# Pair products moved over the loop edge, and a triangular solve by 64x64 blocks in place of the last inversion level

## The chip, the cores and the metric

The kernel runs on one core of one Trainium2 chip. Its time is the device time of one execution, in microseconds. TensorE multiplies matrices, VectorE, ScalarE and GpSimd work on elements, and SyncE issues the transfers between HBM and the core's memory. Each engine works through its own queue in order and waits on semaphores that the others raise.

## The reference

Sixteen sequences of 256 tokens with 128 features pass through two modulated layers. Each layer is an attention-like part and a feed-forward part, both behind a layer norm with shift and scale. In layer 0 these are a selective scan (called `a_` in the kernel) and routed experts (`b_`). In layer 1 they are a gated delta rule with 8 heads (`c_`) and softmax attention with 8 gated experts (`d_`). The change touches the delta rule:

```
def step(S, inp):
    q_t, k_t, v_t, g_t, b_t = inp
    S = S * jnp.exp(g_t)[..., None, None]
    u = (v_t - jnp.einsum('bhk,bhkv->bhv', k_t, S)) * b_t[..., None]
    S = S + jnp.einsum('bhk,bhv->bhkv', k_t, u)
    o_t = jnp.einsum('bhk,bhkv->bhv', q_t, S)
```

The kernel does not step through the tokens. It takes them in two chunks of 128. In a chunk, the vectors `u` of one head solve a system with a 128x128 unit triangular matrix that is made of pair products of keys and of decays. The right-hand side has 32 columns a head.

## The kernel before

The work of one sequence is cut in two. `FIRST_HALF` is the scan, the routed experts and the projections of the delta rule, with the pair products at its end. `SECOND_HALF` is the inversion, its application, the attention and the experts. The loop runs over the sequences, 15 turns: one turn does the first half of sequence i and the second half of sequence i-1. Ahead of the loop stands the first half of sequence 0, behind it the second half of the last sequence. Each engine has a string in `TURNS`, written out by a planner ahead of time, which says for each of its steps whether the next one is of the first half (x) or of the second (y). So the order on an engine is fixed, and a step that waits holds up all that is behind it.

The steps around the change, with their lines:

* `c_gmask` (GpSimd, L552) makes masked decays for a group of four heads; there are four groups. `c_logd` (TensorE, L962) sums them into bank 2, ScalarE takes the exponential (L701), `c_prod` (TensorE, L976) multiplies keys with keys and queries into banks 0 and 1, VectorE multiplies by the decays (L1489, L1491), and `c_unit` (GpSimd, L563, L564) puts ones on the diagonal.
* `c_first` (VectorE, L1499) makes the inverses of the 2x2 blocks. Then six levels double the size of the inverted blocks, from 2 to 128. For both chunks (0 and 1) in turn, a level is a transpose (`lev_T`, VectorE, L1508; the first one L1505), a product of 64x64 tiles (`lev_Z`, L984), an eviction with a mask (L1513), a second product (`lev_TT`, L984) and a copy (ScalarE, L719). The last level works on the block off the diagonal alone, through a full 128x128 inverse `TTf` (L722, L711, L724, L992, L1006, L1019, L1517).
* `c_X` multiplies the whole inverse by the right-hand side `R` (`per_head`, L1034), `c_U` scales it, `c_O`, `c_S` and `c_kS` use it; the second chunk needs the state that the first one leaves.
* `a_norm` to `a_step` prepare the scan. Its eight steps are `drive` (VectorE, L1332), the scan (L1344) and a read (L1352). For each, TensorE spreads one row of B into bank 0 and one of C into bank 1 (L832) and adds up pairs of states (L855), and ScalarE makes the decays (L634).
* `keep_warm` (L1026) are two products whose result nobody reads. They stand ahead of waits of TensorE.

Of the kernel before, what the change touches and what calls it, by code (L numbers as in the profile page):

```python
# [9 lines left out]
ALU = mybir.AluOpType  # L10
ACT = mybir.ActivationFunctionType
# [24 lines left out]
LEVELS = [2, 4, 8, 16, 32, 64]  # L36
# [14 lines left out]
C_GT = C_MERGE + HALF * (len(LEVELS) - 1)  # L51
# [13 lines left out]
def constants():  # L65
# [28 lines left out]
PROJECT = [("c_norm",), ("c_norm2",), ("c_turn",), ("c_ba",), ("c_beta",), ("c_soft",), ("c_soft2",), ("c_gmask", 0), ("c_gmask", 1)]  # L94
PROJECT += [("c_proj", m) for m in range(12)]
PROJECT += [("c_gate",)]
PROJECT += [("c_turn_k", 0), ("c_turn_k", 1), ("c_scales",), ("c_turn_v",), ("c_decay",)]
for gr in range(GROUPS):
    PROJECT += [("c_logd", gr), ("c_prod", gr, 0), ("c_prod", gr, 1), ("c_unit", gr)]
    if gr + 2 < GROUPS:  # L100
        PROJECT += [("c_gmask", gr + 2)]
PROJECT += [("c_roots",)]
# [5 lines left out]
APPLY = [("c_R", 0), ("c_X", 0), ("c_U", 0), ("c_O", 0), ("c_S",), ("c_o", 0), ("c_kS",), ("c_R", 1), ("c_X", 1),  # L108
# [15 lines left out]
SECOND_HALF = INVERT + APPLY + ATTEND + EXPERTS  # L124
# [29 lines left out]
def build(nc, a, out, NB):  # L154
    with ExitStack() as ctx:
# [63 lines left out]
        unit_gate = sb("unit_gate", [P, GROUPS])  # L219
# [58 lines left out]
        gmask = [wide[:, 3, 512 * n:512 * n + 512].rearrange("p (h t) -> p h t", t=P) for n in range(2)]  # L278
        et = [wide[:, 4, 512 * n:512 * n + 512].rearrange("p (h t) -> p h t", t=P) for n in range(2)]
# [21 lines left out]
        inv = sb("inv", [P, 12, 512])  # L301
        TTd = [inv[:, n].rearrange("p (h t) -> p h t", t=HALF) for n in range(2)]
# [31 lines left out]
        released = sem("inversion_step_released")  # L334

# [154 lines left out]
        def _(g):  # L490
# [5 lines left out]
            g.memset(TTf[:], 0.0)  # L496
# [83 lines left out]
        def _(s):  # L580
# [116 lines left out]
            def c_logd(i, gr):  # L697
# [3 lines left out]
                s.activation(et[gr % 2].rearrange("p h t -> p (h t)"), bank(2), ACT.Exp).then_inc(c_et.h, 1)  # L701
# [5 lines left out]
            def lev_T(i, l, ch):  # L707

                if l + 1 == NL:
                    s.wait_ge(c_Tp.h, c_Tp.at(i, ch + 1))  # L710
                    s.copy(TN[ch][0:HALF].rearrange("p h t -> p (h t)"), PS[0:HALF, 5 + ch, :]).then_inc(c_Tl.h, 1)  # L711

            def lev_TT(i, l, ch):
                if l + 2 < NL:
# [3 lines left out]
                if l + 2 < NL:  # L718
# [61 lines left out]
        def _(t):  # L780
# [908 lines left out]
```

## Time and profile before

| what | value |
|---|---|
| median of 3 runs | 3085.35 us (3083.61 to 3086.35) |
| profiled execution | 3073.01 us |
| its span | 3071.2 us |
| TensorE busy | 2502.6 us (81%) |
| VectorE busy | 2245.6 us (73%) |
| ScalarE busy | 1247.8 us (41%) |
| GpSimd busy | 641.2 us (21%) |
| mean granted TensorE clock | 0.906 |

The span goes from the first to the last instruction. The busy share is that of an engine over the whole span. Stretches of one turn of the loop have different limits, so the share alone does not say what a step costs.

### The profile page before, as it was taken

Reading aid. Unit: us, or ns where it says so; the run is one execution under the profiler, and the core shown is the slowest. Engines: PE = TensorE matmul, PEld = TensorE weight load, DVE = VectorE, ACT = ScalarE, POOL = GpSimd, SP = SyncE. Lnnn points to the kernel's source line nnn. Section 1 sums busy time; section 2 is a strip of 40 time slices with the busy share of each in tenths; the row PEclk is TensorE's granted clock in tenths of the full one; section 3 lists DMA queues with packets and bytes.
Section 4 is the critical chain, followed back from the end, with each engine's and each line's share of the span. In section 5 each row is a group of like instructions: output and inputs, shape, how many; then the busy total and the mean of one; then the engine's idle time right before and its main releaser. Section 6 shows DMA issues by size and latency. Waiting matters only on the chain.

```text
span 3071.2 us, 61542 instructions
## 1 busy us (share of the span) xinstructions
PE 2502.6 (81%) x22808; PEld 2004.1 (65%) x22808; DVE 2245.6 (73%) x5056; ACT 1247.8 (41%) x2761; POOL 641.2 (21%) x528
## 2 busy tenths in 40 slices
PE   2477978879887887978889797887988788897897
PEld 1166766757766576766757676575766657676686
DVE  1668777787877778787687877778787777877762
ACT  0233533435344253533425353243534424353342
POOL 0222122131212222122131212313121122202210
PEclk9869989989899898989989998998989989898998
DMA  4000000000000000000000000000000000000000
GB/s 119 2 2 3 2 8 3 7 3 7 2 3 8 2 7 3 6 2 3 7 3 7 2 3 8 3 7 3 7 2 3 7 3 7 3 4 5 1 5 2
DMA packets 24718, 21.52 MB, mean 7 GB/s; under 512 B 7210, under 2 KB 21443, under 8 KB 24403
## 3 DMA queue, kind: packets, MB, share of 16 engines
q1 hardware_dynamic: 24402, 17.14, 2.0%
q8 instruction: 219, 3.59, 0.5%
q14 instruction: 97, 0.79, 0.1%
HBM read 15.00 MB, written 2.13 MB: 6 GB/s over the span
## 4 chain that ended last, share of the span: by engine, by line
PE 60%; DVE 18%; issue 13%; POOL 4%; ACT 3%; SPq 1%; DMA 1%; DVEq 0%; POOLq 0%; ACTq 0%
PE banks L984 8%; PE banks L1160 8%; PE banks L1150 8%; PE banks L1034 6%; PE banks L918 4%; PE banks L927 3%; DVE wide L1332 3%; PE banks L976 3%; DVE wide L1344 2%; PE banks L855 2%; PE banks L962 2%; PE banks L1019 2%; PE banks L1026 2%; PE banks L897 2%; POOL lg L536 2%
## 5 line engine op out<-in xcount | busy, mean ns | idle before, releaser
L532 POOL TENSOR_TENSOR wide<-wide 128x512 f32<-128x512 f32 x128 | 243.5, 1902 | 872.5 <-DVE wide L1352 560.7
L1461 DVE SCALAR_TENSOR_TENSOR wide<-pad,conv,wide 128x256 f32<-128x256 f32 x864 | 389.1, 518 | 0.0
L984 PE MATMUL banks<-inv,mats 64*64 64x64 f32 x5120 | 198.0, 237 | 141.8 <-DVE inv L1505 104.6
L1344 DVE TENSOR_TENSOR_SCAN wide<-wide 128x1024 f32<-128x1024 f32 x128 | 308.4, 2409 | 1.9 <-ACT wide L634 0.3
L634 ACT ACTIVATE wide<-small,a_neg 128x255 f32<-128x255 f32 x512 | 217.8, 497 | 201.8 <-DVE wide L1344 198.9
L984 PEld LDWEIGHTS banks<-inv,mats 64*64 64x64 f32 x5120 | 185.2, 152 | 160.1 <-issue 159.2
L1150 PE MATMUL banks<-inv,up 128*128 128x256 f32 x1024 | 264.9, 387 | 0.0
L1160 PE MATMUL banks<-down,inv 128*128 128x128 f32 x2048 | 257.7, 277 | 0.0
L768 ACT ACTIVATE inv<-banks,up1b 128x256 f32<-128x256 f32 x512 | 215.0, 481 | 105.0 <-PE banks L1150 104.8
L1160 PEld LDWEIGHTS banks<-down,inv 128*128 128x128 f32 x2048 | 249.9, 192 | 5.8
L984 PE MATMUL banks<-inv 64*64 64x64 f32 x5120 | 189.0, 233 | 29.0 <-DVE inv L1513 28.9
L719 ACT COPY inv<-banks 128x512 f32<-128x512 f32 x128 | 74.7, 584 | 333.3 <-DVE inv L1508 332.4
L984 PEld LDWEIGHTS banks<-inv 64*64 64x64 f32 x5120 | 177.3, 147 | 47.9 <-issue 47.4
L1150 PEld LDWEIGHTS banks<-inv,up 128*128 128x128 f32 x1024 | 178.9, 191 | 17.8
L832 PE MATMUL banks<-bc,sel3b 96*128 96x256 bf16 x512 | 104.5, 307 | 83.5 <-DVE wide L1352 59.9
L1026 PE MATMUL banks<-hideb,identb 128*128 128x512 bf16 x512 | 171.6, 420 | 0.0
L855 PE MATMUL banks<-wide,con 128*128 128x512 f32 x256 | 142.8, 653 | 34.0 <-POOL wide L532 34.0
L1332 DVE TENSOR_TENSOR wide<-banks,small 128x1024 f32<-128x1024 f32 x128 | 153.9, 1202 | 19.5 <-PE banks L832 19.5
L563 POOL TENSOR_TENSOR unit_gate<-con 128x1 f32<-128x1 f32 x64 | 12.4, 194 | 732.4 <-DVE mats L1489 732.4
L1352 DVE TENSOR_TENSOR wide<-banks,wide 128x1024 f32<-128x1024 f32 x128 | 155.5, 1215 | 0.5
L1513 DVE TENSOR_TENSOR inv<-banks,con 128x512 f32<-128x512 f32 x160 | 107.2, 686 | 57.4 <-PE banks L984 57.4
L1489 DVE SCALAR_TENSOR_TENSOR mats<-banks,negc,wide 128x128 f32<-128x128 f32 x256 | 77.4, 344 | 98.1 <-PE banks L976 98.1
(281 smaller groups left out, 5160.1 us busy)
## 6 DMA issues: line engine op xcount, KB each, us to landing
gates_bc<-gate_rows SPq DMA_DIRECT2D x32, 128.0 KB, 2.9
up<-in_W SPq DMA_DIRECT2D x1, 2048.0 KB
x<-in_x SPq DMA_DIRECT2D x16, 128.0 KB, 2.1
out<-xn_y SPq DMA_DIRECT2D x16, 128.0 KB, 1.9
wide<-in_wmod SPq DMA_DIRECT2D x2, 384.0 KB
con<-in_con SPq DMA_DIRECT2D x1, 724.0 KB
w_k<-in_Wk SPq DMA_DIRECT2D x1, 512.0 KB
w_q<-in_Wq SPq DMA_DIRECT2D x1, 512.0 KB
```

The costliest lines, as they stand in the source:

```text
L532: g.tensor_tensor(ypart[p % 2], r[:, 0:512], r[:, 512:1024], ALU.add).then_inc(a_yp.h, 1)
L634: last = s.activation(decay[st % 2][:, at + 1:at + T], dt[:, c, 1:T], ACT.Exp, scale=a_neg[:, c, st * SG + q:st * SG + q + 1])
L768: s.activation(hm[e % 2][:, m, :], bank(3 + half, T, q * T), ACT.Relu, bias=up1b[:, HB1 * e + m:HB1 * e + m + 1]).then_inc(d_hid.h, 1)
L855: t.matmul(bank(2), ident, ypart[st % 2], start=st == 2, stop=st == NG + 1).then_inc(a_yq.h, 1)
L984: last = t.matmul(PS[a:b, out, h * HALF:(h + 1) * HALF], weights(h, a, b), values(h, a, b), start=True, stop=True)
L1026: t.matmul(bank(bk), identb[:], hideb[:].unsqueeze(1).broadcast_to([P, HG, P]), start=True, stop=True)
L1034: last = t.matmul(bank(bk, width, first), weights(h), flat[:, first:first + width], start=True, stop=True)
L1150: last = t.matmul(bank(3 + half, T, q * T), up1[:, e, m * P:(m + 1) * P], xxT, start=True, stop=True)
L1160: last = t.matmul(bank(bk, D, j * D), hm[e % 2][:, m, j * P:(j + 1) * P], down1[:, HB1 * e + m, :], start=m == 0, stop=m == HB1 - 1)
L1332: v.tensor_tensor(drive[st % 2].rearrange("p (q c t) -> p q c t", q=SG, c=CB), bank(0).rearrange("p (q t) -> p q t", t=T).unsqueeze(2).bro ...
L1344: v.tensor_tensor_scan(state[st % 2], decay[st % 2], drive[st % 2], 0.0, ALU.mult, ALU.add).then_inc(a_h.h, 1)
L1461: v.scalar_tensor_tensor(dst, src, w, dst, ALU.mult, ALU.add).then_inc(c_conv.h, 1)
```

## The change

* The steps from `c_gmask` to `c_unit` leave the end of the first half and become `PAIRS`, the head of the second. So they move from the end of one turn to the start of the next. `c_roots` stays, and is now ahead of the masks in GpSimd's queue. The masks and the decays move from the scan's memory into `inv`, the logarithms into bank 5 and the products into banks 3 and 4. Four waits are added for what the two halves still share.
* The last level is dropped. The inverse stays as two 64x64 blocks on the diagonal. The top half of the solution is `c_top`: the top block times the top of `R`, and a copy on ScalarE. `c_low` multiplies it by the block off the diagonal, and VectorE adds that to the lower half of `R`. `c_X` then multiplies the lower block by it. `c_low` and `c_X` each have their own `keep_warm`.
* `c_unit` loses the small addition on GpSimd (L563), which gives way to a semaphore.
* All four strings of `TURNS` are new.

```
-LEVELS = [2, 4, 8, 16, 32, 64]
+LEVELS = [2, 4, 8, 16, 32]
...
+PROJECT += [("c_roots",)]
+PAIRS = [("c_gmask", 0), ("c_gmask", 1)]
 for gr in range(GROUPS):
-    PROJECT += [("c_logd", gr), ("c_prod", gr, 0), ("c_prod", gr, 1), ("c_unit", gr)]
+    PAIRS += [("c_logd", gr), ("c_prod", gr, 0), ("c_prod", gr, 1), ("c_unit", gr)]
...
-APPLY = [("c_R", 0), ("c_X", 0), ("c_U", 0), ("c_O", 0), ("c_S",), ("c_o", 0), ("c_kS",), ("c_R", 1), ("c_X", 1),
+APPLY = [("c_R", 0), ("c_top", 0), ("c_low", 0), ("c_X", 0), ("c_U", 0), ("c_O", 0), ("c_S",), ("c_o", 0), ("c_kS",), ("c_R", 1), ("c_top", 1), ("c_low", 1), ("c_X", 1),
...
-SECOND_HALF = INVERT + APPLY + ATTEND + EXPERTS
+SECOND_HALF = PAIRS + INVERT + APPLY + ATTEND + EXPERTS
...
+            def c_top(i, ch):
+                if ch == 1:
+                    keep_warm(4)
...
+                for h in range(NH):
+                    last = t.matmul(PS[0:HALF, 3 + ch, h * DV:(h + 1) * DV], TTd[ch][0:HALF, h, :], R[0:HALF, h, :], start=True, stop=True)
+                last.then_inc(c_tp.h, 1)
+
+            def c_low_(i, ch):
+                keep_warm(7 - ch)
+                t.wait_ge(c_tx.h, c_tx.at(i, ch + 1))
...
+                for h in range(NH):
+                    last = t.matmul(PS[HALF:P, 3 + ch, 256 + h * DV:256 + (h + 1) * DV], MTc[ch][0:HALF, h, HALF:P], top_x[:, h, :],
+                                    start=True, stop=True)
+                last.then_inc(c_lp.h, 1)
```

On ScalarE and on VectorE:

```
+            def c_top(i, ch):
+                s.wait_ge(c_tp.h, c_tp.at(i, ch + 1))
+                s.copy(top_x.rearrange("p h v -> p (h v)"), PS[0:HALF, 3 + ch, 0:256]).then_inc(c_tx.h, 1)
...
+                v.tensor_tensor(R[HALF:P], R[HALF:P], PS[HALF:P, 3 + ch, 256:512].rearrange("p (h v) -> p h v", v=DV),
+                                ALU.add).then_inc(c_low.h, 1)
```

The order that the new strings give, where it matters here (first half plain, second half in brackets). TensorE, from the last projections over the loop's edge: ... c_proj.10 c_proj.11 c_turn_k.0 [d_down.5 d_up.7 d_down.6 d_down.7.0] c_turn_k.1 [d_down.7.1] c_turn_v c_decay | [c_logd and c_prod of all groups] a_turn a_in [levels 0 and 1] a_xproj a_dt [level 2, lev_Z.3] a_scan.0 [lev_TT.3] a_read.0 a_scan.1 a_read.1 a_scan.2 [level 4] a_read.2 a_scan.3 a_read.3 [c_top.0 c_low.0] a_scan.4 [c_X.0] a_read.4 a_scan.5 [c_O.0 c_S] a_read.5 a_scan.6 [c_kS] a_read.6 a_scan.7 a_read.7 [c_top.1] a_scan.8 a_read.8 [c_low.1 c_X.1] a_scan.9 a_read.9 [c_O.1] a_out b_turn b_logits [c_turn_o c_out] b_coef b_up.0 to b_up.3 [d_turn] b_up.4 [d_qkv] b_up.5 [d_scores] b_out [d_turn_p d_av d_a] c_turn [d_gates d_up.0.0] c_ba and so on.

VectorE: ... c_proj.11 [d_mix.4] c_scales [d_mix.5 to d_mix.7 d_res] | a_norm a_norm2 [c_prod of all groups, c_first.0] a_conv [c_first.1, level 0, lev_T.1.0] a_zgate [rest of level 1] a_silu2 [lev_T.2] a_split [lev_Z.2.0] a_soft [lev_Z.2.1 lev_T.3] a_step [lev_Z.3.0] a_scan.0 [lev_Z.3.1] a_read.0 a_scan.1 [lev_T.4] a_read.1 a_scan.2 [lev_Z.4] a_read.2 a_scan.3 a_read.3 [c_R.0] a_scan.4 [c_low.0] a_read.4 [c_U.0] a_scan.5 [c_o.0] a_read.5 a_scan.6 a_read.6 a_scan.7 [c_R.1 c_low.1] a_read.7 [c_U.1] a_y [c_o.1] a_res b_norm [c_rms] b_norm2 b_logits [c_gated] b_soft2 b_select b_coef [c_res] b_up with [d_norm] and [d_norm2] between, then [d_v d_max d_prob] b_res and so on.

Before, level 4 was through ahead of a_scan.0 on VectorE, the last level stood between a_scan.0 and a_scan.2, c_R.1 and c_U.1 had a_scan.6 between them, c_o.1 was ahead of a_read.7, d_scores ahead of b_up.1, and d_turn_p ahead of b_out.

## Rows read from the trace of the kernel before

**Rows 1.** Timeline of SyncE's queue: start us, us, what; the stores.

```profile
384.74 0.41 SPq L461 DMA_DIRECT2D out<-xn_y  x1
...
1664.46 0.41 SPq L461 DMA_DIRECT2D out<-xn_y  x1
...
1845.77 0.41 SPq L461 DMA_DIRECT2D out<-xn_y  x1
...
2941.33 0.40 SPq L461 DMA_DIRECT2D out<-xn_y  x1
```

**Rows 2.** Windows of one turn: from:to, length, busy per engine, TensorE's clock, DMA.

```profile
1494.70:1500.40 5.70, 0.00 (x0) 0.00 (x0) 3.63 (x7) 0.00 (x0) 5.70 (x3) 0.62 0.02 6
...
1534.50:1582.20 47.70, 37.39 (x297) 28.75 (x295) 45.53 (x43) 15.51 (x35) 18.80 (x10) 0.88 0.00 1
...
1615.60:1664.30 48.70, 48.70 (x326) 44.27 (x325) 40.38 (x112) 35.05 (x83) 3.63 (x3) 1.00 0.00 1
```

**Rows 3.** Timeline of VectorE around the loop's edge: start us, us, engine line.

```profile
1504.77 0.48 DVE L1219 BATCH_NORM_STATS2 stats_x<-x 128x6 f32<-128x128 f32 x2
...
1506.60 0.61 DVE L1231 TENSOR_SCALAR xn_x<-x,mv_x 128x128 f32<-128x128 f32 x2
...
1663.86 0.42 DVE L1242 TENSOR_TENSOR xn_y<-x,inv 128x256 f32<-128x256 f32 x1
...
1668.35 0.61 DVE L1489 SCALAR_TENSOR_TENSOR mats<-banks,negc,wide 128x128 f32<-128x128 f32 x2 [2.90 <-PE banks L976]
...
1678.22 0.41 DVE L1491 TENSOR_TENSOR mats<-banks,wide 128x256 f32<-128x256 f32 x1
```

**Rows 4.** Line L1499 (`c_first`) of the whole run: releaser of idle time, us, times.

```profile
  issue: 28.2, 14
```

**Rows 5.** Timeline of TensorE at the head of a turn.

```profile
1666.06 1.10 PE L962 MATMUL banks<-wide,con 128*128 128x512 f32 x2
...
1684.36 3.37 PE L984 MATMUL banks<-inv,mats 64*64 64x64 f32 x64 [6.75 <-DVE inv L1505]
...
1700.88 1.10 PE L817 MATMUL banks<-small,w_bc 128*96 128x256 f32 x4 [0.45 <-DVE small L1294]
```

**Rows 6.** Timeline of ScalarE at the loop's edge and ahead of the scan.

```profile
1492.01 0.60 ACT L701 ACTIVATE wide<-banks 128x512 f32<-128x512 f32 x1 [2.20 <-PE banks L963]
1492.50 0.40 ACT L705 COPY x_kept<-x 128x256 f32<-128x256 f32 x1
...
1526.49 1.28 ACT L622 ACT_TABLE_LOAD   x1
```

**Rows 7.** Timeline of VectorE in the scan: first drives and a last read.

```profile
1534.54 1.23 DVE L1332 TENSOR_TENSOR wide<-banks,small 128x1024 f32<-128x1024 f32 x1 [1.13 <-PE banks L832]
...
1576.81 1.21 DVE L1352 TENSOR_TENSOR wide<-banks,wide 128x1024 f32<-128x1024 f32 x1
...
1716.44 1.23 DVE L1332 TENSOR_TENSOR wide<-banks,small 128x1024 f32<-128x1024 f32 x1 [1.13 <-PE banks L832]
```

**Rows 8.** Timeline of TensorE, scan to the end of a turn.

```profile
1537.13 1.09 PE L992 MATMUL banks<-con,TTf 64*64 64x64 f32 x16
...
1572.14 1.97 PE L1034 MATMUL banks<-inv,mats 128*128 128x128 f32 x16
...
1601.09 1.03 PE L1095 MATMUL banks<-inv 128*128 128x256 f32 x4
...
1615.63 1.11 PE L1150 MATMUL banks<-inv,up 128*128 128x256 f32 x4
...
1663.29 1.07 PE L935 MATMUL banks<-con,kq 128*128 128x128 f32 x8
```

**Rows 9.** Chain that ended last, behind the loop: start us, us, what.

```profile
2959.59 12.23 PE banks L984 x321
...
2981.94 0.58 ACT TTf L722
...
2989.46 0.59 ACT TTf L724
```

More of the change, by code:

```diff
@@ L50 @@
 C_MERGE = C_MASK2 + HALF
[L51 removed]
+C_GT = C_MERGE + HALF * len(LEVELS)
 C_LE = C_GT + 128
@@ L93 @@
 ROUTED += [("b_up", m) for m in range(BLK0 + 1)] + [("b_out",), ("b_res",)]
[L94 removed]
+PROJECT = [("c_norm",), ("c_norm2",), ("c_turn",), ("c_ba",), ("c_beta",), ("c_soft",), ("c_soft2",)]
 PROJECT += [("c_proj", m) for m in range(12)]
@@ L773, in _ @@
                            c_turn=lambda i: modulate(i, 2, 0), c_beta=c_beta, c_soft=lambda i: sp_exp(i, 1), c_proj=c_proj,
-                           c_turn_k=c_turn_k, c_turn_v=c_turn_v, c_decay=c_decay, c_logd=c_logd, lev_T=lev_T, lev_TT=lev_TT,
+                           c_turn_k=c_turn_k, c_turn_v=c_turn_v, c_decay=c_decay, c_logd=c_logd, lev_TT=lev_TT, c_top=c_top,
                            keep_x=keep_x, c_S=c_S_, c_turn_o=c_turn_o, d_turn=lambda i: modulate(i, 3, 7), d_qkv=d_qkv, d_exp=d_exp,
@@ L797, in turn_x @@
                     keep_warm(7)
+                if n == 0 and not isinstance(i, int):
+                    t.wait_ge(c_vtok.h, c_vtok.at(i - 1, 1))
                 t.wait_ge(ln_x[n].h, ln_x[n].at(i, 1))
@@ L806, in a_in @@
                 t.wait_ge(ln_h[0].h, ln_h[0].at(i, 1))
+                if not isinstance(i, int):
+                    t.wait_ge(c_eGS.h, c_eGS.at(i - 1, 1))
                 for c in range(CB):
@@ L1014, in lev_TT @@
                 t.sem_inc(released, 1)
-                if l + 2 < NL or l + 2 == NL:
-                    last = halves(5 + ch, lambda h, a, b: WW[ch][a:b, h, :], lambda h, a, b: TTd[ch][a:b, h, :])
-                else:
-                    for h in range(NH):
-                        last = t.matmul(PS[0:HALF, 5 + ch, h * HALF:(h + 1) * HALF], WW[ch][HALF:P, h, :], TTf[HALF:P, ch, h, HALF:P],
-                                        start=True, stop=True)
-                last.then_inc(c_TTp.h, 1)
+                halves(5 + ch, lambda h, a, b: WW[ch][a:b, h, :], lambda h, a, b: TTd[ch][a:b, h, :]).then_inc(c_TTp.h, 1)
             def keep_warm(bk):
@@ L1167, in _ @@
                            c_turn=lambda i: turn_x(i, 2, 0), c_ba=c_ba_, c_proj=c_proj, c_turn_k=c_turn_k, c_turn_v=c_turn_v,
-                           c_decay=c_decay, c_logd=c_logd, c_prod=c_prod, lev_T=lev_T, lev_Z=lev_Z, lev_TT=lev_TT, c_X=c_X_,
+                           c_decay=c_decay, c_logd=c_logd, c_prod=c_prod, lev_Z=lev_Z, lev_TT=lev_TT,
+                           c_top=c_top, c_low=c_low_, c_X=c_X_,
                            c_O=c_O_, c_S=c_S_, c_kS=c_kS_, c_turn_o=c_turn_o, c_out=c_out_, d_turn=lambda i: turn_x(i, 3, 7),
@@ L1642, in _ @@
                            c_norm=lambda i: norm(i, 2), c_norm2=lambda i: norm2(i, 2), c_beta=c_beta, c_soft2=c_soft2,
-                           c_proj=c_proj, c_scales=c_scales, c_prod=c_prod, c_first=c_first, lev_T=lev_T, lev_Z=lev_Z, c_R=c_R_, c_U=c_U_,
+                           c_proj=c_proj, c_scales=c_scales, c_prod=c_prod, c_first=c_first, lev_T=lev_T, lev_Z=lev_Z, c_R=c_R_, c_low=c_low_, c_U=c_U_,
                            c_o=c_o_, c_rms=c_rms_, c_gated=c_gated, c_res=c_res, d_norm=lambda i: norm(i, 3),
```

122 lines of the change are left out of this document (50 added, 72 removed).

## The prediction, as put on record

> **What bounds the kernel now.** I read the stores first: they give the period of the loop. From the first to the fifteenth are 2556.6 us for 14 turns, 182.6 us each, in two kinds that alternate, 181.3 and by difference 183.9 [rows 1]. Then the windows of one turn [rows 2]. The last stretch is full: TensorE is busy for all of its 48.7 us. In the scan stretch VectorE is busy 45.5 of 47.7 us. Between pair products and inversion TensorE does nothing for 5.7 us. So a turn is a row of stretches with different limits, and I cost the change stretch by stretch. T is the end of a turn's last residual: 1664.28 us in one turn [rows 3], 183.9 earlier, 1480.4, in the turn before.
>
> In the kernel before, the products run alone behind T: VectorE does them from T+4.1 to T+14.35, and the first block product of the inversion starts at 1684.36, T+20.1 [rows 3, 5]. The scan's first `drive` starts at T+52.2 in this turn and at T+54.1 in the one before, whose last read ends at 1578.02 and whose first expert product starts at 1615.63 [rows 7, 8].
>
> **Stretch 1, T to the first block product: +1.9 us.** The loop's back edge moves. VectorE now jumps back between `d_res` and `a_norm`; before, between `c_prod` and `c_first`, where it stood 2.0 us for "issue", 14 times in 16 [rows 4]; that is every turn entered by a jump and neither of the two reached without one. ScalarE shows nothing of the kind: `keep_x`, its first step after the jump, starts before the exponential ahead of it has ended, at 1492.61 [rows 6]. So the price at the new place lies between 0 and 2.0; I take 2.0, the row of the same engine. Then `a_norm` and `a_norm2`, with GpSimd's power between them, take 2.4 [rows 3], so the first product's eviction is at T+4.4. TensorE would be ready earlier: evictions began 2.3 us after `c_logd.0` [rows 3, 5], and that step now starts about T-0.25, since one sum of squares and two turns went ahead of the last expert product (below). The evictions last 10.3 us as before and end at T+14.7. Behind them in VectorE's queue are `c_first.0` (1.4), then a wait for `a_turn`, `a_in` and the copy to the pad, which now stand behind all products in TensorE's queue (until T+16.6), the convolution (3.2, my estimate from its eight 128x256 instructions at about 0.4), `c_first.1` and a transpose: first block product at T+22.0. The cover is poor: `a_norm` to `a_conv` are hidden no better, they go in front.
>
> The Trainium skill, "Runtime: NRT & Kernel Launch", section Instruction fetch mechanics, says that a taken branch whose target lies outside the two pages held makes the engine wait for a fetch. VectorE's row agrees, ScalarE's does not. By that rule TensorE pays too, which would still be hidden behind VectorE's 4.4 us; by ScalarE's row the sum would be 1.9 us a turn lower, and that is the second rival.
>
> **Stretch 2, to the scan's start: -11.0 us.** Here lies the gain. Alone, the inversion runs at TensorE's pace: five half-levels, with a slow first one, in 12.23 us [rows 9]; level 0 at the low clock costs 5.5 (its first two products 3.37 [rows 5]), level 1 4.5. Behind it `a_xproj` (2.1 for two parts like the 1.10 of [rows 5]) and `a_dt` (1.1) now stand next to each other with ScalarE's copies (0.8) between, and the level-2 products wait behind both: they start 14.05 us after the first block product. From there the x chain decides: a product, `a_soft` (with the product's eviction 2.9), exponential, table load (1.28 [rows 6]), logarithm (2.55 in all), `a_step` and an eviction (2.1): 22.1 us. Before it was 32.1, and by the turn before, counted from T+20.1, 34.0 [rows 5, 7], mean 33.1, since levels 3 and 4 came ahead of the scan.
>
> **Stretch 3, scan start to its last read: +7.8 us.** Before 43.5 [rows 7]. VectorE is full here, so each second-half instruction put in it counts. Removed: the last level's two copies (1.3) and `c_o.1` (1.4), the latter only moved. Added: an eviction of level 3, two transposes and two evictions of level 4, two `c_low`: net +0.8. Then waits, because the scan's spread of B for the next step stands in TensorE's queue behind second-half work. At scan 3 the two last inversion products and a read are ahead of it: 0.7. At scan 4, `c_top.0` and `c_low.0` are ahead, with ScalarE's copy between them: from the right-hand side on, a 0.95 product, 0.35, a 0.95 product and the spread, against 2.2 of scan: 1.9. Around `c_S`: 0.5. Worst, `c_R.1` and `c_low.1` are next to each other in VectorE's string, while TensorE has between them the scan's sum 7, two fills, `c_top.1`, the scan's sum 8, two fills and `c_low.1`: 0.7+0.6+0.9+1.0+0.6+0.9 = 4.7, of which I take 4.5. The last read, which is ready, is queued behind it. Less 0.6 of waits before. Sum +7.8.
>
> The price of the small products: eight heads, one 64x64 tile each, 32 columns wide. The nearest row is such a product with 64 columns, 1.09 us for sixteen instructions [rows 8]; half of it is the lower bound, if columns decide. I take 0.95, because even 128x128 transposes at 0.13 an instruction [rows 8] are not cheap by their size. Per solve: removed one 128x128 `c_X` (1.97, as in [rows 8]), added top, low and X of 0.95 and two further pairs of fills.
>
> The Trainium skill, "TensorEngine Tiling (Array Packing)", section Instruction Overhead, says that a product with one column takes as long as one with 60. By it each small product costs the 64-column row's 1.09; by columns alone 0.55, and stretch 3 would be some 1.6 us shorter.
>
> **Stretch 4, last read to the experts' first product: +5.2 us.** Before 37.6 [rows 7, 8]. `c_O.1` (0.6 of fills and 1.97 [rows 8]) now stands ahead of `a_out`, and `c_gated` ahead of the softplus: +1.15 until the experts of the first layer are selected. `b_up` is no longer, since `d_norm` and `d_norm2` lie in its gaps. But `d_qkv` and `d_scores` (1.03 [rows 8]) with ScalarE's copies are now ahead of `b_out`: it starts 2.2 later. Behind `b_out` the attention still has `d_turn_p`, a copy, `d_av` and `d_a` to go, where before only the last two were left: +1.45. Gates +0.4.
>
> **Stretch 5, to the next T: +1.4 us.** TensorE is full here before [rows 2] and stays so. The last sum of squares (0.79) and `c_turn_k` (1.07 [rows 8]) come into it, ahead of T instead of behind it; `c_turn` (0.4) goes out. VectorE has 40.4 of 48.7 to do [rows 2], so it could add a wait; I take none.
>
> Moved without price: `c_gmask` and `c_unit` on GpSimd (idle there; two roots of 2.9 end before the masks are wanted), SyncE's queue (no transfer is touched), the level-4 copies on ScalarE (whole banks, shorter). The cover for the first mask is the 8 us of expert products behind `c_scales`; without it, 7 us.
>
> **Sum.** +1.9 - 11.0 + 7.8 + 5.2 + 1.4 = +5.3 us a turn, 79.5 in 15 turns. At the end, without a scan, the change gains: from the copy at 2981.94 to the copy at 2989.46 the last level took 7.5 us plus 2.7 of copy and product [rows 9]; top, copy, low, add and X take 5.0, and 2.0 more in the second solve: -3.2. The pair products leave the prologue and come back behind the loop: nothing. The profiled execution took 3073.01 (span 3071.2 and 1.8 around it), so 3149; the median of the three runs is 3085.35, 12.3 above it, and I set the forecast beside that: 3085.4 + 76.3 = 3162 us, 2.5% slower.
>
> **Rivals.** (a) Faster: the waits of stretch 3 do not come, because the small products and ScalarE's copy are through before VectorE wants the next B. For it speaks that second-half work between scan steps costs VectorE next to nothing before (2.2 idle in 47.7, [rows 2]); against it that no block there held a round trip to ScalarE. Place: `c_top`/`c_low`. Price: 7.6 of waits; without them -2.3 a turn, 3085 - 34.5 - 3 = 3047. It decides when the waits together are under 2.3 us. Chance 0.20. (b) The jump costs nothing at its new place: T+20.1, +3.4 a turn, 3133; by itself still slower. Chance 0.15. (c) Waits halved, and `a_xproj`'s stall covered: +1.5 a turn or less, 3105, at its lower edge no change: 0.15. (d) The low clock spreads: TensorE idles some 8 us more a turn, and one more level at half rate costs 1.4 to 2.7: 3162 + 21 to 41, about 3195; for it, a clock of 0.62 in the 5.7 us of idleness [rows 2]. Chance 0.12. The forecast itself (3140 to 3185): 0.38.
>
> **Range and chances.** About 0.2% (6 us) is what a measurement can tell from no change. Faster holds (a) and nothing else: 0.20, with 0.01 from the rest. Same: the edge of (c), 0.05. Slower: 0.74. The range goes from 3050, inside (a), to 3205, beyond (d); if it is slower, 3105 to 3200.
>
> **What would show it.** In the profile after: 2 us of "issue" ahead of VectorE's first statistics; the scan starting at T+44; VectorE waiting 4 to 5 us for TensorE ahead of the second `c_low`, and near 2 for the spread after the first; the last 50 us with TensorE full; TensorE's idle time up by 8 us a turn. If the waits around `c_low` are under 1 us each, the forecast is wrong by its largest term; if the scan starts later than T+48, by its only gain.

## The result: slower by 8.7%, and the profile after

The changed kernel takes 3354.61 us (median of 4 runs, 3350.59 to 3356.87), the kernel before 3085.41 beside it: a ratio of 1.0872 with a 95% interval of 1.0853 to 1.0891, 269 us more. The forecast was 3162 us, 3050 to 3205. The direction holds, the size does not: 77 us more were forecast, 3.5 times as many came, and the time lies far outside the range.

The stores again give the period of the loop. Timeline of SyncE's queue in the changed kernel:

```profile
1616.40 0.41 SPq L463 DMA_DIRECT2D out<-xn_y  x1
...
1817.74 0.41 SPq L463 DMA_DIRECT2D out<-xn_y  x1
```

One turn is 201.3 us, against 181.3 or 183.9 before [rows 1], and the two kinds of turn are gone. Windows of this turn in the changed kernel, cut at the same five marks as in the prediction (from:to, length, then the busy time of TensorE, its weight loads, VectorE, ScalarE and GpSimd, each with its count, TensorE's clock, share of the DMA engines, GB/s):

```profile
1616.30:1639.87 23.57, 15.44 (x55) 10.61 (x55) 15.82 (x46) 4.43 (x8) 5.58 (x9) 0.93 0.06 18
1639.87:1662.13 22.26, 19.94 (x464) 17.30 (x464) 14.99 (x27) 7.84 (x13) 0.00 (x0) 0.92 0.01 3
1662.13:1717.65 55.52, 43.02 (x410) 31.86 (x410) 43.73 (x39) 16.83 (x40) 14.47 (x7) 0.75 0.00 1
1717.65:1767.30 49.65, 38.07 (x139) 23.26 (x139) 24.04 (x88) 9.85 (x23) 10.19 (x7) 0.69 0.01 3
1767.30:1817.64 50.34, 49.68 (x336) 45.27 (x335) 40.02 (x117) 35.66 (x85) 9.20 (x5) 1.00 0.01 1
```

Two things are to be seen. The last stretch is full of TensorE work as before [rows 2], so the loss isn't there. And in the two stretches before it the granted clock is 0.75 and 0.69, where the scan's window of before had 0.88 [rows 2]; VectorE is busy 43.7 of 55.5 us in the scan, where it was 45.5 of 47.7 in a window of before that reached a little beyond the scan's last read.

Where one turn's time goes, as means over the 14 turns between stores in each profile, from the starts in the timelines: 1 is from the store (just behind the last residual) to the first block product, 2 to the scan's first `drive`, 3 to the end of its last read, 4 to the experts' first product, 5 to the next store.

| us per turn | 1 | 2 | 3 | 4 | 5 | sum |
|---|---|---|---|---|---|---|
| before | 19.9 | 33.1 | 43.5 | 37.3 | 48.8 | 182.6 |
| forecast change | +1.9 | -11.0 | +7.8 | +5.2 | +1.4 | +5.3 |
| after | 23.4 | 21.8 | 56.3 | 49.6 | 50.4 | 201.5 |
| measured change | +3.5 | -11.3 | +12.8 | +12.3 | +1.6 | +18.9 |

The gain, stretch 2, came as forecast. Stretches 3 and 4 together lost 12.1 us more than forecast. The scan on VectorE in the changed kernel (a bracket is the idle time ahead, and who ended it):

```profile
1691.84 1.23 DVE L1322 TENSOR_TENSOR wide<-banks,small 128x1024 f32<-128x1024 f32 x1 [3.55 <-PE banks L830]
...
1695.59 0.42 DVE L1541 TENSOR_TENSOR inv<-banks,cU 128x256 f32<-128x256 f32 x1 [0.81 <-PE banks L1033]
...
1701.92 0.42 DVE L1549 TENSOR_TENSOR inv<-banks,rq 128x256 f32<-128x256 f32 x1 [2.13 <-PE banks L1002]
...
1715.97 0.42 DVE L1534 TENSOR_TENSOR inv<-inv,banks 64x256 f32<-64x256 f32 x1 [3.80 <-PE banks L1024]
```

And TensorE in the same stretch:

```profile
1687.00 1.45 PE L1016 MATMUL banks<-inv 64*64 64x32 f32 x16
1688.38 1.03 PE L994 MATMUL banks<-hideb,identb 128*128 128x512 bf16 x2
1689.35 1.92 PE L1024 MATMUL banks<-inv,mats 64*64 64x32 f32 x16
1691.19 0.61 PE L830 MATMUL banks<-bc,sel3b 96*128 96x256 bf16 x2
...
1714.82 1.11 PE L1024 MATMUL banks<-inv,mats 64*64 64x32 f32 x16
```

The spread that VectorE waits 3.55 us for (L830) stands behind `c_top.0`, a pair of fills and `c_low.0`. The sixteen small products of `c_low` take 1.92 us at 1689 and 1.11 at 1714: the first run at the lower of the clock's two levels (1.2 GHz), the second at the higher (2.4).

Behind the scan, one line each over the whole run, the routed half's first layer (L875 here, L877 in the kernel before; min/median/max in ns). First the changed kernel, then the kernel before:

```profile
L875 PE MATMUL banks<-hT_x,up x160: 631/634/796, 140.9 to 3163.5; 128*128 128x256 f32 x128, 128*64 128x256 f32 x32
```

```profile
L877 PE MATMUL banks<-hT_x,up x160: 379/379/796, 140.5 to 2882.7; 128*128 128x256 f32 x128, 128*64 128x256 f32 x32
```

Not one of the 160 is faster than 631 ns in the changed kernel; before, at least half took 379, and 134 of them less than 500.

### The profile page after: what moved, and what is told of

It reads as the page before. It is cut to its first block, busy times and chain, and to the rows that moved or that the text cites. A ratio compares the mean times of both kernels' runs of the same rounds, so it can differ in the third digit from the quotient of the medians.

```text
span 3352.8 us, 60529 instructions
## 1 busy us (share of the span) xinstructions
PE 2690.2 (80%) x22424; PEld 2063.7 (62%) x22424; DVE 2225.2 (66%) x5056; ACT 1198.9 (36%) x2697; POOL 627.1 (19%) x463
## 3 DMA queue, kind: packets, MB, share of 16 engines
HBM read 15.00 MB, written 2.13 MB: 5 GB/s over the span
## 4 chain that ended last, share of the span: by engine, by line
PE 67%; DVE 13%; issue 11%; ACT 5%; POOL 3%; SPq 1%; DMA 1%; ACTq 0%; DVEq 0%; POOLq 0%
PE banks L976 8%; PE banks L1149 7%; PE banks L1139 6%; PE banks L1002 5%; PE banks L968 4%; PE banks L853 3%; PE banks L994 3%; PE banks L916 3%; PE banks L925 3%; PE banks L875 3%; PE banks L830 2%; PE banks L881 2%; PE banks L958 2%; DVE wide L1334 2%; DVE wide L1342 2%
## 5 line engine op out<-in xcount | busy, mean ns | idle before, releaser
L1454 DVE SCALAR_TENSOR_TENSOR wide<-pad,conv,wide 128x256 f32<-128x256 f32 x864 | 370.5, 500 | 0.0
L1334 DVE TENSOR_TENSOR_SCAN wide<-wide 128x1024 f32<-128x1024 f32 x128 | 292.1, 2282 | 4.1 <-ACT wide L635 4.1
L976 PE MATMUL banks<-inv,mats 64*64 64x64 f32 x5120 | 213.9, 250 | 82.1 <-DVE inv L1498 81.4
L976 PEld LDWEIGHTS banks<-inv,mats 64*64 64x64 f32 x5120 | 201.5, 164 | 102.4 <-issue 100.7
L994 PE MATMUL banks<-hideb,identb 128*128 128x512 bf16 x640 | 246.2, 475 | 0.0
L830 PE MATMUL banks<-bc,sel3b 96*128 96x256 bf16 x512 | 120.6, 347 | 146.4 <-DVE wide L1342 118.6
L713 ACT COPY inv<-banks 128x512 f32<-128x512 f32 x160 | 91.0, 577 | 282.6 <-DVE inv L1501 185.2
L853 PE MATMUL banks<-wide,con 128*128 128x512 f32 x256 | 174.6, 783 | 21.6 <-POOL wide L533 21.6
L830 PEld LDWEIGHTS banks<-bc,sel3b 96*128 96x128 bf16 x512 | 47.1, 118 | 216.9 <-DVE wide L1342 133.3
L1630 DVE SCALAR_TENSOR_TENSOR inv<-banks,gt,inv 128x128 f32<-128x128 f32 x256 | 78.0, 348 | 110.5 <-PE banks L1149 108.5
```

The source lines that it names most:

```text
L830: last = t.matmul(bank(bk, T, q * T), sel3b[:, row + q:row + q + 1].broadcast_to([3 * 2 * NS, P]), bc3[:], start=True, stop=True)
L853: t.matmul(bank(2), ident, ypart[st % 2], start=st == 2, stop=st == NG + 1).then_inc(a_yq.h, 1)
L976: last = t.matmul(PS[a:b, out, h * HALF:(h + 1) * HALF], weights(h, a, b), values(h, a, b), start=True, stop=True)
L994: t.matmul(bank(bk), identb[:], hideb[:].unsqueeze(1).broadcast_to([P, HG, P]), start=True, stop=True)
L1334: v.tensor_tensor_scan(state[st % 2], decay[st % 2], drive[st % 2], 0.0, ALU.mult, ALU.add).then_inc(a_h.h, 1)
L1454: v.scalar_tensor_tensor(dst, src, w, dst, ALU.mult, ALU.add).then_inc(c_conv.h, 1)
```

## The experiments

All times of kernels sent together stand beside runs of the kernel before on the same chip; the comparison is by ratio, and "us" is that ratio's excess times 3085. The orders are given as they run in the loop: x steps are the first half, y steps the second (in brackets where both stand in one line). The columns 1 to 5 are the stretches, in us per turn, from each kernel's profiled execution.

| kernel | ratio (95%) | us | 1 | 2 | 3 | 4 | 5 |
|---|---|---|---|---|---|---|---|
| the change | 1.0872 (1.0853 to 1.0891) | +269 | 23.4 | 21.8 | 56.3 | 49.6 | 50.4 |
| e1_old_order | 1.0676 (1.0652 to 1.0700) | +209 | 25.5 | 29.6 | 49.0 | 44.0 | 48.8 |
| e2_pairs_only | 1.0167 (1.0122 to 1.0212) | +52 | 25.7 | 29.9 | 44.1 | 37.3 | 48.8 |
| e3_blocks_only | 1.0518 (1.0494 to 1.0541) | +160 | 20.0 | 32.4 | 49.5 | 43.9 | 48.8 |
| e4_more_fills | 1.0838 (1.0817 to 1.0858) | +259 | 23.0 | 22.1 | 56.2 | 48.5 | 50.4 |
| e5_blocks_slots | 1.0078 (1.0059 to 1.0098) | +24 | 20.0 | 32.5 | 45.7 | 37.9 | 48.8 |
| e6_slots_fills | 1.0080 (1.0058 to 1.0102) | +25 | 20.0 | 32.4 | 46.1 | 37.5 | 48.8 |
| e7_both_slots | 1.0245 (1.0224 to 1.0266) | +76 | 26.1 | 29.5 | 45.4 | 37.9 | 48.8 |
| e8_late_tail | 1.0448 (1.0413 to 1.0482) | +138 | 20.4 | 29.1 | 45.4 | 46.5 | 50.4 |
| e9_early_front | 1.0899 (1.0881 to 1.0917) | +277 | 28.9 | 22.1 | 55.7 | 45.6 | 48.8 |
| e10_full_fills | 1.0633 (1.0609 to 1.0657) | +195 | 23.3 | 22.2 | 55.8 | 44.3 | 50.5 |
| e11_blocks_trim | 1.0062 (1.0045 to 1.0080) | +19 | 19.9 | 32.3 | 45.2 | 38.1 | 48.8 |
| e12_own_ends | 1.0050 (1.0036 to 1.0063) | +15 | 20.0 | 29.4 | 45.5 | 37.8 | 51.9 |
| e13_pairs_own_ends | 0.9975 (0.9965 to 0.9985) | -8 | 20.3 | 29.5 | 44.0 | 37.4 | 51.9 |

### Taking the change apart

**e1_old_order.** Both parts, TensorE's order in the scan:

```diff
-y: lev_Z.3.1  x: a_scan.0  y: lev_TT.3.0 lev_TT.3.1  x: a_read.0 a_scan.1 a_read.1 a_scan.2
-y: lev_Z.4.0 lev_Z.4.1 lev_TT.4.0 lev_TT.4.1  x: a_read.2 a_scan.3 a_read.3
-y: c_top.0 c_low.0  x: a_scan.4  y: c_X.0 ...
+y: lev_Z.4.1 lev_TT.4.0  x: a_scan.0  y: lev_TT.4.1  x: a_read.0 a_scan.1  y: c_top.0
+x: a_read.1 a_scan.2  y: c_low.0  x: a_read.2 a_scan.3  y: c_X.0  x: a_read.3 a_scan.4
+y: c_O.0 c_S ...  (behind the scan: as in the kernel before)
```

> The changed kernel's whole structure (pair products at the head, right-hand side by 64x64 blocks, five levels), but from the scan on with the order of the kernel before in each string: the levels all lie ahead of the scan, one step of the block solve sits between two scan steps, and everything behind the scan stands as it stood before. Theory 'order': what the changed kernel lost in its scan stretch (+12.0 us a turn) and behind it (+12.05) comes from its strings. Then only the head's +3.5 us a turn is left, less about 1.6 us for the VectorE work of the sixth level: +1.9 x 15, so 3115 us (3080 to 3150). Theory 'structure': the solve's five round trips in place of one product and the unhidden head cost what they cost in any order: 3300 us or more, near the changed kernel's 3355.

**e2_pairs_only.**

```diff
-SECOND_HALF = INVERT + APPLY + ATTEND + EXPERTS
+SECOND_HALF = PAIRS + INVERT + APPLY + ATTEND + EXPERTS
 LEVELS = [2, 4, 8, 16, 32, 64]
```

> Only the pair products moved to the head of the second half (with their buffers, banks and waits); all six levels and the one product for the right-hand side stay, and the rest of the strings keeps the order of the kernel before. Theory 'order': the price is the loop edge on TensorE and VectorE and the first products at the low clock, the +3.5 us that the first stretch lost, so 3085 + 15 x 3.5 = 3138 us (3110 to 3165). Theory 'structure': the head is the heavy part, and this alone takes a good half of the loss: 3220 us or more.

**e3_blocks_only.**

```diff
-LEVELS = [2, 4, 8, 16, 32, 64]
+LEVELS = [2, 4, 8, 16, 32]
 SECOND_HALF = INVERT + APPLY + ATTEND + EXPERTS
```

> Only the right-hand side solved by 64x64 blocks and no sixth level; the pair products stay at the end of the first half, and the strings keep the order of the kernel before, with one step of the solve between two scan steps. Theory 'order': VectorE loses about four instructions and gains two half ones in a stretch that it fills, some -1.6 us a turn: 3061 us (3030 to 3090). Theory 'structure': round trips between TensorE, ScalarE and VectorE in the scan stretch make it longer by 5 us a turn or more: 3160 us or more.

Measured: +209, +52 and +160 us. e2 and e3 add up to e1 (212 and 209), and the pairs alone cost about what "order" said. But e1 and e3 are far from its numbers and near those of "structure". What e3 waits for speaks against taking that as the answer. Its VectorE in the scan:

```profile
1638.83 0.42 DVE L1535 TENSOR_TENSOR inv<-banks,cU 128x256 f32<-128x256 f32 x1 [1.47 <-PE banks L1030]
...
1647.02 0.42 DVE L1543 TENSOR_TENSOR inv<-banks,rq 128x256 f32<-128x256 f32 x1 [2.12 <-PE banks L999]
...
1663.83 0.42 DVE L1528 TENSOR_TENSOR inv<-inv,banks 64x256 f32<-64x256 f32 x1 [2.25 <-PE banks L1021]
```

Each is the eviction of a product that my order had put one scan step too near. In the kernel before, `c_U.0` comes after its scan step's read; here it came in front. The second chunk's solve also ended later: its last product stood behind `a_scan.9`, in the kernel before behind `a_scan.6`. Both can be undone without touching the structure.

### The same parts, laid out anew

**e5_blocks_slots**, TensorE (its reads left out) and VectorE (up to the first chunk's end) against e3_blocks_only:

```diff
 TensorE
-a_scan.1 [c_top.0] a_scan.2 [c_low.0] a_scan.3 [c_X.0] a_scan.4 [c_O.0 c_S] a_scan.5 [c_kS]
-a_scan.6 [c_top.1] a_scan.7 [c_low.1] a_scan.8 [c_X.1] a_scan.9 [c_O.1]
+a_scan.1 [c_top.0 c_low.0] a_scan.2 [c_X.0] a_scan.3 [c_O.0 c_S] a_scan.4 [c_kS]
+a_scan.5 [c_top.1 c_low.1] a_scan.6 [c_X.1 c_O.1]
 VectorE
-a_scan.2 [c_low.0] a_read.2 a_scan.3 [c_U.0] a_read.3 a_scan.4 [c_o.0] a_read.4
+a_read.1 [c_low.0] a_scan.2 a_read.2 [c_U.0] a_scan.3 a_read.3 [c_o.0] a_scan.4 a_read.4 [c_R.1]
```

> As e3_blocks_only (pairs at the end of the first half, block solve, five levels), with the solve laid into the scan's slots anew: the first two steps of each chunk's solve share one slot between two scan steps, the products behind them stand where they stood in the kernel before, VectorE takes each result only after the read of its step, and everything from the scan's seventh step on is as before. Theory 'slots': the 6 us a turn that e3_blocks_only's scan stretch was longer are waits of VectorE for products that this order put one slot too close (2.25, 2.12, 1.47, 0.85, 0.71 us and three of 0.6), so this lands near the kernel before: 3080 us (3060 to 3100). Theory 'clock': the sixth level and the 128-wide product were what raised TensorE's clock inside the scan (in the kernel before it is at its high level from 1552 on, 17 us into the scan; in e3_blocks_only a fill of two still takes 1.06 us 27 us into it), so VectorE waits whatever the slots: 3150 us or more.

**e6_slots_fills:**

```diff
 def c_top(i, ch):
-    if ch == 1: keep_warm(4)
+    keep_warm(4, 2 if ch == 1 else 4)
 def c_X_(i, ch):
-    keep_warm(7 - ch)
+    keep_warm(7 - ch, 2 if ch == 1 else 4)
```

> As e5_blocks_slots, with four fill products ahead of the first chunk's first solve product (none stood there) and four in place of two ahead of its last one. Theory 'slots': the same time as e5_blocks_slots, within 5 us. Theory 'clock': the fills raise TensorE's clock early in the scan, and this is faster than e5_blocks_slots by 2 to 4 us a turn, 30 to 60 us.

**e7_both_slots:** the order of e5_blocks_slots with the pair products at the head.

> The changed kernel's whole structure with the order of e5_blocks_slots from the levels on and the pair products at the head as in e2_pairs_only. The two parts added up so far (54 + 160 = 214 us beside the 208 us of e1_old_order), so this is e5_blocks_slots plus 54 us: 3135 us if theory 'slots' holds, 3200 us or more if 'clock' does.

Measured: +24, +25 and +76 us. The same instructions as in e3_blocks_only, in other slots, are 136 us cheaper; as in e1_old_order, 133. Nearly all of the block solve's price was where its steps stood. By stretches, e5 wins 3.8 us a turn in the scan, where the waits of VectorE went, and 6.0 behind it, where the second chunk now comes three scan steps earlier; no run takes the two moves apart. With 3105 us e5 is still just above the range of "slots", and far from "clock". e6 shows no gain: fills early in the scan don't help. e7 is the whole change for +76 instead of +269, so **193 us of the change's loss are its own strings**.

### Which of its strings

**e8_late_tail:** e7_both_slots to the end of the scan, then the changed kernel's order (VectorE: `a_y a_res b_norm c_rms b_norm2 b_logits c_gated b_soft2 b_select b_coef c_res b_up.0 b_up.1 d_norm` and so on).

> e7_both_slots up to the end of the scan, and behind it the changed kernel's own order: the routed half's steps run to their end with the second half's output norm, output projection and attention held back between and behind them. Theory 'tail': stretch 4 (last read to the first product of the experts) is longer in the changed kernel because of this order alone: 37 becomes 49, stretch 5 48.8 becomes 50.4, 3157 + 15 x 13.4 = 3358 us (3320 to 3370), the changed kernel's time. Theory 'late': stretch 4 is long because the last chunk's solve, its output product and norm come only after the scan: with those early, as here, the order behind costs little, 3157 to 3230 us.

**e9_early_front:** the changed kernel's order to the end of the scan, then that of e7_both_slots.

> The other way round: the changed kernel's own order up to the end of the scan (scan begun with two levels to go, the last chunk's output product behind the scan), and behind it the order of e7_both_slots and of the kernel before. Theory 'tail': stretch 4 falls from 49.6 to 37 to 44 us (44 is what e1_old_order and e3_blocks_only took with a solve that ended one slot late), stretches 1 to 3 stay 101 us together, and 5 is 48.8: 3355 - 15 x (5.7 + 1.6) = 3245 us, 3150 at best. Theory 'late': stretch 4 keeps 47 us or more: 3300 us or more.

Stretch 4: 37.9 in e7, 46.5 in e8, 45.6 in e9, 49.6 in the change. Each half alone brings most of it: the order behind the scan 8.6 us, the late last chunk 7.7, both 11.7. Both theories are half right, though the whole times (3214 and 3359 us) lie where "late" had them: e9's is that long because its stretch 1 is 28.9 us, which "What the head costs" explains. The two halves cost in different ways. In e8 none of the 160 products of the routed half's first layer takes less than 500 ns, as in the change; in e9 121 of them do, before 134. So the low clock there came with the order behind the scan, and the late chunk costs its 7.7 us with that layer mostly at the high clock. The front also shows that the early scan is no gain: stretches 2 and 3 together are 78.1 us in the change, 74.9 in e7. What stretch 2 wins, stretch 3 gives back with 3 us on top.

**e4_more_fills** and **e10_full_fills** change nothing but fills behind the scan, in the changed kernel:

```diff
 def turn_x(i, n, bk):
+    if n == 1: keep_warm(7, 6)      # e10: 14
 def b_coef(i):
+    keep_warm(3, 6)                 # e10: 14
```

> The changed kernel with six more fill products in each of the two TensorE idle stretches behind the scan (3.96 us ahead of the routed half's transposes and 3.98 us ahead of its coefficient transposes), nothing else. Theory 'clock': the routed half's five steps run at 1.22 us for each product because TensorE was idle just before them; with the fills they run at 0.69, 4 x 0.75 us less a turn and some more on the products behind the scan, so about -4 us a turn, 3295 us (3280 to 3320). Theory 'waits': the low clock only fills slots in which TensorE would wait for VectorE anyway: 3350 to 3360 us.

> e4_more_fills with fourteen fills in place of six at each place; there the six took 1.5 and 1.8 us of gaps of 4, left 2.4 to 2.7 us idle, and the routed half's products still took 1.22 us. Theory 'clock': with the gaps full these products take 0.69 and stretch 4 loses 3 to 4 us more, 3335 - 50 = 3285 us (3270 to 3305). Theory 'waits': 3325 to 3345 us, as e4_more_fills.

e4 came out at +259, 10 us below the change and with an interval that touches its own: inconclusive, since gaps of about 2.7 and 2.2 us were left. e10 gives 74 us back (3274 us, within the range of "clock"), in stretch 4 (49.6 to 44.3), with more work on TensorE. Its line for the first layer:

```profile
L877 PE MATMUL banks<-hT_x,up x160: 379/483/796, 138.6 to 3081.9; 128*128 128x256 f32 x128, 128*64 128x256 f32 x32
```

The median falls from 634 to 483 ns. The granted clock of stretch 4, as a mean over the 14 turns, is 0.84 in e10, as in the kernel before, and 0.69 in the change. So the low clock behind the scan is a cause, worth at least 5.3 of the 12.3 us, and not only a filler of waits; the other 7.0 us stay with the clock back at its old mean.

**e11_blocks_trim:** e5_blocks_slots with `c_o.0` behind `a_scan.4` and without `keep_warm(7)` ahead of `c_S`.

> e5_blocks_slots with its two waits in the scan taken out: VectorE's first output step goes one place later (it waited 0.99 us there for a product that took 2.7 us), and the fill ahead of the state product goes (a spread was 0.81 us late behind it). Theory 'slots': 1.8 us a turn less, 3105 - 27 = 3078 us (3070 to 3090), level with the kernel before. Theory 'clock': without the fill the slots behind run slower, 3100 us or more.

+19 us where level was expected, which the intervals do not tell from e5's +24: stretch 3 goes from 45.7 to 45.2 only. VectorE in that kernel still waits for a spread:

```profile
1757.26 1.23 DVE L1318 TENSOR_TENSOR wide<-banks,small 128x1024 f32<-128x1024 f32 x1 [1.49 <-PE banks L821]
```

### What the head costs

Stretch 1 is 25.7 in e2 and 26.1 in e7, but 20.4 in e8, with the same head. The difference is the end of the turn. GpSimd and TensorE at the edge in e7_both_slots:

```profile
1707.40 2.90 POOL L509 TENSOR_TENSOR vscale<-vscale,expo 128x16 f32<-128x16 f32 x1 [38.52 <-DVE rq L1461]
1710.26 2.89 POOL L509 TENSOR_TENSOR rq<-rq,expo 128x16 f32<-128x16 f32 x1
1713.12 2.03 POOL L551 TENSOR_TENSOR inv<-gl,con 128x512 f32<-128x512 f32 x2
...
1714.21 2.08 PE L956 MATMUL banks<-inv,con 128*128 128x512 f32 x2 [5.44 <-POOL inv L551]
```

and in e8_late_tail:

```profile
1742.10 2.89 POOL L509 TENSOR_TENSOR rq<-rq,expo 128x16 f32<-128x16 f32 x1
1744.96 2.04 POOL L551 TENSOR_TENSOR inv<-gl,con 128x512 f32<-128x512 f32 x2
...
1750.36 1.49 PE L956 MATMUL banks<-inv,con 128*128 128x512 f32 x2 [2.54 <-issue]
```

The masks (L551) stand behind two powers in GpSimd's queue, and those wait for `c_scales`. In e7 that step comes after the turn's last residual, and TensorE waits 5.44 us for the first mask; in e8 it comes three blends earlier, and only the 2.54 us of "issue" are left. e9, with the changed kernel's head and the late `c_scales`, waits for the mask too: 28.9 us in stretch 1 against the change's 23.4.

> e7_both_slots (both parts, scan laid out anew, the order of the kernel before up to the experts' first product), with the changed kernel's own order from the experts' first product to the end of the turn. There VectorE computes the scales three expert blends earlier, so GpSimd's two powers of 2.9 us and the first two masks are done before the turn ends. Theory 'roots queue': stretch 1 falls from 25.3 to 26.4 to 20.1 us, as in e8_late_tail, and stretch 5 rises from 48.8 to 50.45: 4.6 us a turn less, 3157 - 69 = 3088 us (3070 to 3095). Theory 'edge': the extra 5.5 us of the first stretch are the loop edge of the head, whatever stands at the end of the turn: 3150 to 3180 us.

> e2_pairs_only (six levels, one product for the right-hand side, pair products at the head) with the changed kernel's own order from the experts' first product to the end of the turn. Theory 'roots queue': the same 4.6 us a turn less than e2_pairs_only, 3133 - 69 = 3064 to 3080 us: the pair products at the head then cost nothing beside the kernel before. Theory 'edge': 3125 to 3160 us.

```diff
 VectorE, end of the turn
-d_mix.5 c_proj.10 d_mix.6 c_proj.11 d_mix.7 d_res c_scales
+c_proj.10 c_proj.11 d_mix.4 c_scales d_mix.5 d_mix.6 d_mix.7 d_res
```

Stretch 1 falls to 20.0 and 20.3 us, and the two kernels to +15 and -8: "roots queue" holds for both. Stretch 5 came out at 51.9 rather than 50.4, because work moved into it, so stretches 1 and 5 together are 3.0 us (e12 against e7) and 2.3 us (e13 against e2) shorter and not 4.6; some 10 us more come behind the loop, where the first block product starts that much sooner. e12 is a little above its range. The head on VectorE in e13_pairs_own_ends:

```profile
1859.00 0.49 DVE L1218 BATCH_NORM_STATS2 stats_x<-x 128x6 f32<-128x128 f32 x2 [2.55 <-issue]
```

The jump is still there, and stretch 1 is 20.3 us against 19.9 before all the same. e13, the pair products moved and six levels kept, is the fastest kernel here: 3077.6 us (median of 9), 0.25% below the kernel before, little more than the 0.2% that the prediction took for the least that can be told; its profiled execution, at 3087.88, was the slowest of the nine. The block solve on top of it (e12) costs 23 us, and in the loop it gains no more than 0.3 us in any stretch. Behind the loop, where no scan shares the queues, it seems to gain: from the loop's last store to the experts' first product e12 takes 88.0 us and e13 92.5; but e5 and the kernel before, the same comparison without the moved pairs, take 93.6 and 93.4.

## Why the prediction was wrong, step by step

**Stretch 1, +1.9 forecast, +3.5 measured.** Both engines at the head of the changed kernel:

```profile
1618.76 0.49 DVE L1209 BATCH_NORM_STATS2 stats_x<-x 128x6 f32<-128x128 f32 x2 [2.53 <-issue]
...
1622.05 0.61 DVE L1482 SCALAR_TENSOR_TENSOR mats<-banks,negc,inv 128x128 f32<-128x128 f32 x2 [0.82 <-PE banks L968]
```

```profile
1618.55 1.33 PE L958 MATMUL banks<-inv,con 128*128 128x512 f32 x2 [2.74 <-issue]
...
1620.10 3.20 PE L968 MATMUL banks<-kq 128*128 128x256 f32 x8
...
1639.87 2.40 PE L976 MATMUL banks<-inv,mats 64*64 64x64 f32 x40 [5.09 <-DVE inv L1498]
```

VectorE's jump was taken at 2.0 and took 2.53. I let TensorE's be hidden; it stood 2.74 us, and the first products ran at the low clock (the first eight pair products took 3.20 us, later groups of eight 1.89), so the first eviction came at T+5.8 instead of T+4.4. The convolution in VectorE's queue ahead of the second chunk, forecast at 3.2, took 3.1: e8, with the same head but that convolution behind both chunks, has 20.4 instead of 23.4. The Trainium skill's "Runtime: NRT & Kernel Launch", Instruction fetch mechanics, which the prediction weighed, has an engine wait for a fetch when it takes a branch to a target outside the two pages held. The trace agrees on VectorE and TensorE; ScalarE's row of before shows no wait [rows 6], and in the changed kernel its first step behind the jump waits for TensorE, so nothing can be read there.

**Stretch 2, -11.0 forecast, -11.3 measured.** Right.

**Stretch 3, +7.8 forecast, +12.8 measured.** The mechanism was right and its size off. VectorE's work grew by about the 0.8 us forecast; the term that was too small is "waits". In the turn of the windows above VectorE is idle 55.5 - 43.7 = 11.8 us, where 7.6 were forecast. The wait ahead of the second `c_low` was 3.80, forecast 4.5. That for the spread behind `c_top.0` and `c_low.0` was 3.55, forecast 1.9: its small products were priced at 0.95 and took 1.45 and 1.92 at the low clock. And the waits "around `c_S`: 0.5" were 2.13 and 0.81. I costed every product of this stretch at the high level, while the mean granted clock of the stretch is 0.73 (0.88 before). How much of the 5.0 us too little the clock makes, and how much the order, no run separates: fills were added only behind the scan and, in e6, early in it. At the high level the 64x32 products take 1.08 to 1.11 us for sixteen, like those with 64 columns [rows 8], and my 0.95 was too low. "TensorEngine Tiling (Array Packing)", Instruction Overhead, in the Trainium skill says that a product with one column takes as long as one with 60; these rows agree.

**Stretch 4, +5.2 forecast, +12.3 measured: the step that failed.** I summed what moved ahead of `a_out` and `b_out`, at the high clock, and put the chain of the routed half's first layer between them at nothing. TensorE in the changed kernel:

```profile
1721.77 3.46 PE L1002 MATMUL banks<-inv,mats 128*128 128x128 f32 x16
...
1742.41 0.60 PE L887 MATMUL banks<-con,cf 128*9 128x128 f32 x2 [3.98 <-DVE cf L1384]
1742.80 1.06 PE L875 MATMUL banks<-hT_x,up 128*128 128x256 f32 x2
1743.79 1.22 PE L881 MATMUL banks<-cfT,con 8*128 8x256 f32 x2
1744.94 1.22 PE L875 MATMUL banks<-hT_x,up 128*128 128x256 f32 x2
...
1758.41 1.47 PE L895 MATMUL banks<-down,wide 128*128 128x128 f32 x10
```

and in the kernel before:

```profile
1594.66 0.69 PE L800 MATMUL banks<-con,xn_y 128*128 128x128 f32 x2 [3.96 <-DVE xn_y L1231]
...
1596.15 2.07 PE L1085 MATMUL banks<-hT_y,at_w 128*128 128x256 f32 x4
...
1599.13 0.39 PE L889 MATMUL banks<-con,cf 128*9 128x128 f32 x2 [0.27 <-DVE cf L1394]
...
1602.48 0.69 PE L883 MATMUL banks<-cfT,con 8*128 8x256 f32 x2
...
1608.02 1.57 PE L897 MATMUL banks<-down,wide 128*128 128x128 f32 x10 [0.48 <-DVE wide L1414]
```

Windows of the chain itself, from the coefficients' transposes to the end of the last `b_up`, first in the changed kernel, then in the kernel before (columns as above):

```profile
1742.40:1754.30 11.90, 11.89 (x25) 5.05 (x26) 5.95 (x19) 4.12 (x9) 0.70 (x1) 0.50 0.00 0
```

```profile
1599.10:1607.00 7.90, 7.59 (x29) 3.93 (x30) 5.31 (x15) 4.66 (x14) 0.00 (x0) 1.00 0.00 0
```

In this turn and the one of the prediction stretch 4 grew by 12.0 us, in three parts. Its first part, to the coefficients' transposes (L887, L889 before), is 24.76 us against 21.11, +3.65 where 1.15 were forecast; the last output product, in the forecast at 1.97 us, took 3.46. From there to the first product of `b_out` (L895, L897 before) it is 16.00 against 8.89, +7.11 where 2.2 were forecast. The last part is 8.89 against 7.61, +1.28 where 1.85 were forecast (1.45 and 0.4).

So the term that failed is in the middle part: "`b_up` is no longer, since `d_norm` and `d_norm2` lie in its gaps", a price of nothing. From the coefficients' transposes to the end of the last `b_up` the changed kernel takes 4.5 us more. In the kernel before, TensorE stood idle for 3.96 us too, but behind that came the second half's transposes, a pair of fills and the projections, and only then the coefficients, at a granted clock of 1.00. In the changed kernel these stand behind `b_up.3` and later steps, so TensorE came out of 3.98 us of idleness straight into the chain, and each link ran at the low level, a granted clock of 0.50.

For the whole stretch e10 gives the clock at least 5.3 us. e8 and e9 show that the order behind the scan brings 8.6 by itself and the late last chunk 7.7, and that the low clock of the chain goes with the first of the two. These numbers overlap and can't be added.

**Stretch 5, +1.4 forecast, +1.6 measured.** Right. Outside the loop -3.2 us were forecast. The two profiled spans differ by 281.6 us, of which 15 turns at the mean of 14 make 283.1, so about -1.5 came.

**The rivals.** (a) was wrong for these strings; e5 shows what it described, waits that nearly go, with the steps in other slots (VectorE idle for 2.6 us a turn in stretch 3, where the change has 12.6), and even there the kernel is not faster. (b) and (c) didn't occur. (d), "the low clock spreads", occurred and was priced too low: 1.4 to 2.7 us a turn, with a chance of 0.12, where e10 gave 5.3 back in stretch 4 alone. It is a part of the excess of 13.6 us a turn and not all of it: that the late second chunk and the waits of stretch 3 could cost more than forecast stood in no rival. The range was built from terms at one clock, and its upper end stood on (d) at half its size or less.

**Still open.** The 1.7 us by which stretch 3 stays longer with the block solve in its best order here (45.2 in e11 against 43.5): as means over the 14 turns VectorE is busy for 43.0 us there and 42.7 before, idle for 2.2 and 0.8, and the granted clock is 0.79 and 0.88. The spread's wait of 1.49 is in the trace, but the one test with fills (e6) moved nothing. Whether a better order exists wasn't tried.

## What to carry to other kernels

When a chain is broken into smaller steps inside a full pipeline, the number of steps can cost less than the place of each: give every product a whole step of the other chain before its result is wanted, and let the last one end no later than it did (the two together 136 us of 160 here). Price each moved product at both clock levels, and ask of every gap on TensorE what stood in it: here work taken from a gap left the chain behind it at the low clock. And when work is put at the head of a loop, look at what its first operand is queued behind on the slow engine, one turn earlier.

## What the runs showed of the hardware that I had not expected

- TensorE pays at the loop's jump too: in the changed kernel's 14 turns 2.32 to 2.84 us of "issue", VectorE 2.53 to 2.88. ScalarE's row of before shows nothing [rows 6].
- GpSimd's power of a 128x16 tile takes 2.89 us, of a 128x2 tile 0.70: it grows with the columns, though not in proportion.
- A pair of fills takes 1.06 us at the low level of the clock and 0.60 at the high. Six fills in each of two gaps near 4 us covered 1.5 and 1.8 to 2.0 us of them, fourteen 3.2 and 3.7 in one turn. Of the routed half's 160 products 8 took less than 500 ns with six fills, 110 with fourteen, none in the change and 134 in the kernel before.
